# Attention of a graph network: GpSimd's gathers wait for TensorE's sums, in place of VectorE's weighting

## What is computed

```
ft   = (hn @ W_att).reshape(n, 10, 13)
ft_s, ft_d = ft[src], ft[dst]
scores = einsum('ehd,ehd->eh', ft_s, ft_d) / sqrt(13)
ex  = exp(scores - segment_max(scores, dst)[dst])
agg = segment_sum(ft_s * (ex / z[dst])[:, :, None], dst)
out = layer_norm(elu(agg) @ hr_w + hr_b + h_skip) ...
```

## Time and profile before

| | |
|---|---|
| median of three runs | 4847.91 us |
| profiled execution | 4847.73 us |
| its span, first to last instruction | 4845.9 us |
| busy: TensorE, VectorE, ScalarE, GpSimd | 4130.6, 2183.2, 1864.7, 1504.7 us |
| share of the span | 85%, 45%, 38%, 31% |
| first and last gather start | 118.3 us, 2909.2 us |

### The profile page before, as it was taken

One profiled execution on the slowest core, in us unless ns is written; L12 is line 12 of the kernel. 1 busy time (PEld: TensorE's weight loads), 2 busy tenths in 40 slices (PEclk: granted clock), 3 DMA queues, 4 the chain that ended last, 5 costly groups with the idle time before them and its releaser, 6 DMA issues. The chain is left out here.

```text
span 4845.9 us, 61839 instructions
## 1 busy us (share of the span) xinstructions
PE 4130.6 (85%) x21902; PEld 2401.5 (50%) x21902; DVE 2183.2 (45%) x3396; ACT 1864.7 (38%) x5147; POOL 1504.7 (31%) x1605
## 2 busy tenths in 40 slices
PE   5478888888888887787888786889999999999999
PEld 4245555555555555555555554544454445445444
DVE  7366666666666666666666664750011002002000
ACT  4455555555555555555555553650001002002000
POOL 2555555555555555555555550000000000000000
PEclk7577677767667677767676767999999999999999
DMA  6232222222222222222222224126665665665665
GB/s 199 61 80 74 74 74 73 74 74 75 73 75 73 76 72 76 72 76 72 76 72 76 72 76 83 35 90 198 208 191 181 208 196 174 208 196 181 209 204 169
DMA packets 467250, 560.45 MB, mean 116 GB/s; under 512 B 45449, under 2 KB 411684, under 8 KB 466686
## 3 DMA queue, kind: packets, MB, share of 16 engines
q1 hardware_dynamic: 383558, 366.63, 24.8%
q0 software_dynamic: 51168, 107.68, 10.5%
q10 hardware_dynamic: 32248, 82.62, 4.4%
HBM read 455.16 MB, written 103.20 MB: 115 GB/s over the span
## 5 line engine op out<-in xcount | busy, mean ns | idle before, releaser
L897 POOL DMA_INDIRECT fts<-ft_tab,src_all x1568 | 1482.1, 945 | 1309.9 <-DVE terms L971 890.0
L2161 PE MATMUL cv_acc<-cv_cnt,cv_parts 128*128 128x512 bf16 (+1 forms) x7056 | 1431.3, 366 | 0.0
L2161 PEld LDWEIGHTS cv_acc<-cv_cnt,cv_parts 128*128 128x128 bf16 x7056 | 666.0, 98 | 761.6
L1078 ACT CAST strip<-adj_ps 128x392 bf16<-128x392 f32 x784 | 373.2, 476 | 1118.4 <-remote 707.4
L948 DVE TENSOR_TENSOR prod<-ftd_ps,fts 128x780 f32<-128x780 f32 (+1 forms) x392 | 274.2, 700 | 1062.1 <-issue 678.2
L934 DVE TENSOR_TENSOR ohk<-iota_ps,key_cols 128x784 bf16<-128x784 f32 x784 | 722.7, 960 | 3.1
L1192 PE MATMUL agg_ps<-terms,oh 128*64 128x141 f32 x2744 | 675.6, 436 | 5.1 <-DVE terms L971 5.1
L1126 PE MATMUL adj_ps<-own,own_low 32*128 32x392 bf16 x784 | 311.1, 397 | 421.6 <-ACT strip L1078 396.5
L1996 DVE TENSOR_TENSOR cv_y<-cv_acc,dis_row 128x512 f32<-128x512 f32 (+1 forms) x52 | 34.4, 661 | 1355.2 <-PE cv_acc L2161 1326.5
L1192 PEld LDWEIGHTS agg_ps<-terms,oh 128*64 128x64 f32 x2744 | 585.3, 222 | 55.7 <-issue 37.4
L1130 PE MATMUL adj_ps<-ohk,ohl 128*128 128x196 bf16 x3136 | 544.6, 305 | 67.4 <-issue 65.5
(11 more groups left out here) (264 smaller groups left out, 2964.9 us busy)
## 6 DMA issues: line engine op xcount, KB each, us to landing
cv_cnt<-adj SPq DMA_DIRECT2D x96, 2048.0 KB, 8.3
cv_cnt<-adj SPq DMA_DIRECT2D x48, 2176.0 KB, 8.6
adj<-strip ACTq DMA_DIRECT2D x196, 392.0 KB
fts<-ft_tab,src_all POOLq DMA_INDIRECT x1568
win<-ft_tab SPq DMA_DIRECT2D x196, 65.0 KB
agg_tab<-res SPq DMA_DIRECT2D x196, 35.2 KB
cv_cnt<-adj SPq DMA_DIRECT2D x8, 512.0 KB, 3.7
agg_tab<-zero_f SPq DMA_DIRECT2D x10, 352.5 KB
```

Of the source, the lines that this page charges most:

```text
L897: nc.gpsimd.indirect_dma_start(fts[u][:, k, :], None, ft_tab[:, :], bass.IndirectOffsetOnAxis(src_all[:, n, k:k + 1], 0)).then_inc(gathere ...
L1078: nc.scalar.copy(strip[:, k.s, :, QS * q:QS * (q + 1), :].rearrange("p t a d -> p a t d"), adj_ps[q % 2][:, 0:QS * KEYS].rearrange("p (a t ...
L2161: last = nc.tensor.matmul(a[:, 0:width], parts[:, r, b, :], cnt[q][:, 0:width // SUB, (b - b0) * SUB:(b - b0 + 1) * SUB], start=(b == 0 an ...
```

## The change

The wait of GpSimd ahead of a group's gathers is on the semaphore `agg_done` in place of `terms_done`, with the same number. `agg_done` rises once per group, at the end of TensorE's last sum (L1204), which reads `terms` of that group and so comes behind it. Nothing else differs: every engine has the same instructions in the same order.

```diff
             for n in range(NG):
                 u = n % FU
                 if n >= FU:
-                    pool.wait_ge(terms_done, n - FU + 1)
+                    pool.wait_ge(agg_done, n - FU + 1)
                 for k in range(GC):
                     nc.gpsimd.indirect_dma_start(fts[u][:, k, :], None, ft_tab[:, :],
```

## The result

The changed kernel takes **5017.4 us** (median of four, 5006.66 to 5032.28) where the kernel before takes 4849.44 (four, 4844.19 to 4852.31) beside it: 1.0353 of it, 95% interval 1.0331 to 1.0375. It is slower; the forecast was 4384, with a range up to 4720. What came is rival (c), in price (5030 forecast) and, as the rows show, in its mechanism: the second `ftd` of every other group is caught.

The account below looks back on a forecast made before the run. It took the attention to be bound by a ring of waits on TensorE's reports, held during GpSimd's gathers. 190 periods x (14.24 - 11.8) = 464 us less: 4848 - 464 = 4384 us, range 4250 to 4720.

Parts of the forecast that it names:

- rival (c): Attention stage: the hold reaches TensorE's second `ftd`; every other period 18.5 us, mean 15.2, time 5030; chance 0.14.
- What bounds the kernel now: Attention stage: a ring of waits; during GpSimd's gathers TensorE's reports are held, released 1.9 us after the last; period 14.24.
- The new ring, 11.8 us: Attention, per group: last sum's report, 0.27 us to first gather, 9.70 of gathers, 1.9 to release: 11.87, taken as 11.8.
- Does the rest fit in 11.8?: Attention group: other engines' work fits in 11.8 us; second `ftd` has 2.3 us of margin before the hold at +6.3.
- the onset: In a burst of gathers, TensorE's reports begin to be held between +6.3 and +8.0 us after the burst's start.
- The start should lead into this state: At the stage's start the first burst moves behind the first group's sums, and each next one starts on a release.
- What the profile should show: GpSimd's idle before L897 put to `agg_ps` L1204; burst and first `prod` within 0.3 us; second `prod` near +4; clock above 0.71.
- signs of failure: Attention stage: alternating periods, second `prod` starting at +11, or last gather to first `prod` no longer near 2 us.
- Rival (d): Attention stage: no change; the hold isn't GpSimd's, or costs its 3.8 us wherever it falls; 4848 us; chance 0.08.

Follow-up runs that it names:

- e8: Changed kernel, its first burst of a used buffer (group 6) also waiting once for the first `prod` of group 3; 4828.12 us, kernel before 4818.27.
- e1: Kernel before, with gathers for the first six groups alone, all others weighing the rows that lie in the buffers; 3902.82 us, kernel before 4851.29.
- e5: Kernel before, with eight plain transfers of the same size, issued by GpSimd, replacing a group's gathers behind the sixth group; 3907.01 us, kernel before 4851.29.

## Why the prediction was wrong

By its own steps:

- **What bounds the kernel now: right.** A ring of waits with TensorE's late reports in it. The experiments bear the reading out: without indirect gathers, with spread ones, or on another chip, the waits are gone.
- **The new ring, 11.8 us: right where it applies.** Bursts follow each other at 11.94 us in the short half. The release comes 1.8 us behind the last gather (1651.81 against 1650.03), as before.
- **"Does the rest fit in 11.8?": the step that failed.** It gave the second `ftd` 2.3 us of margin, because in the earlier trace rows a report at +6.3 of a burst was still prompt. In the changed kernel the first late one ended at +3.5, and the second `ftd` at +4.8 (+4.7 in e8, the state set by hand). Rival (c) named just this condition, "less than 4 us after a burst's start", and the price, a mean of 15.2; measured 15.1. I gave it 0.14. That the two means agree so well is in part luck: (c) has first `prod`s 18.5 and 11.8 us apart, and they are 17.04 and 13.65 above: the first is shorter because the burst starts 1.1 us ahead of the first `prod`, the second longer by a wait that (c) left out, TensorE's 3.17 us for late strips.
- **Why the onset was misread.** I took it for a span of time from the burst's start, and laid earlier onsets to a lack of rest. That isn't it: the burst of 1640.36 began after 9.13 us of rest and held reports from +3.5. The rows differ in another way. In the opening burst TensorE had little to report. From 1640.36 to 1643.85 it finished two parts of `ftd`, two quarters of `adj_ps`, the spread maxima and a `near_ps`. Nor are the late ones all kept to the end: one is seen in mid-burst at 1647.52 here, two in turn at 131.80 and 133.93 in the opening burst, and the rest together when the gathers end. (The `strip` at 1649.08 says less: ScalarE was busy with `ohl` until then.) That could be a queue that close gathers slow down rather than a door that shuts: reports are late when more came than it passes, and a burst on top of a busy stretch of TensorE meets it sooner. It stays a guess. No run measured such a rate, and the counts don't give one: in the burst of 1640.36 six reports pass before the first late one, in the opening burst three (a `near_ps` of L1139, one of L1144, a quarter of `adj_ps`). What the rows do show is that the onset isn't one time from the burst's start. Either way the place of a burst matters: in the kernel before it starts at +2.52 of `prod`, so that the second `ftd` is out at +1.5 of the burst.
- **"The start should lead into this state": wrong as well.** The first burst moved as said (214.02, behind a sum), and the alternation was there from the next one on. e8 set the start by hand and lost the state too, so a better start would not have saved the forecast; how much of the 3.5% hangs on the start stays open (e8 took 0.2% more than the kernel beside it).
- **What the profile should show: half right.** The idle time ahead of L897 is put down to `agg_ps` L1204. But the burst and the first `prod` don't start together (the burst of 1640.36 is 1.1 us ahead of one, that of 1652.30 6.2 us), the second `prod` left +4, the mean clock fell to 0.68 (from 0.71) where it was to rise, and both signs of failure that were named came: alternating periods, and a second `prod` at +10.3 (1651.81 against 1641.49).
- **Rival (d)** fell with e1 and e5. The rule it cites, of the Trainium skill, SBUF — State Buffer, "Who interferes with whom", that "PE and ACT never wait on anyone", speaks of the engines' ports to SBUF. The rows agree in so far as TensorE's matmuls run on beside the gathers. What waits is everyone who is to hear of them, and on two of the chips nobody does.

**Still open:** why some chips hold reports and others don't (three sets with the hold, two without, each on another chip; a state of the chip at the time isn't told apart from the chip), by what way gathers delay reports, and how much of the 3.5% hangs on the start of the stage. The `iota` that spaces the gathers was not tried at sizes between 128 and 384, nor with the changed wait on a chip with the hold.

## What to carry to other kernels

A wait that looks local can set the phase of a burst, and where the burst disturbs its neighbours the phase is what you pay for: before you move a release, list which results of other engines end in each microsecond of the new overlap, and ask it of the results that the moved burst now covers, not of its old place. A limit read as "from +6.3 us on" out of one stretch with little traffic is one point, not a threshold. And measure on more than one chip: here one edit reads 1.035 on one and 1.000 on another, and a spacing of the gathers 0.943 or 1.132.

## What the runs showed of the hardware

- On some chips, GpSimd's indirect gathers that follow at 1.25 us hold back TensorE's completion reports, by 3.7 to 6.7 us in the steady group above, up to 1.8 to 2.3 us behind the last gather. Gathers 1.60 us apart don't, nor do plain transfers of the same bytes on the same queue (a period of 9.27 against 14.24), though those bursts are also less than half as long.
- It depends on the chip, or on its state: the same kernel takes 4818 to 4851 us in three sets and 3985 to 3989 in two, with gathers of 945 and 946 ns and TensorE's rows alike in the opening burst. That is a factor of 1.2 in time between chips, far over the 0.2% between the runs of this kernel on one.
- A gather costs GpSimd 0.94 us and 0.30 of pause in both cases, the same as before and after the change, so nothing in its own rows betrays the hold; the neighbours' idle time under "remote" and "issue" does.
